# A two-layer transformer kernel in fp32 on one core: block 1 of the feed-forward part joins the seven-product scheme, with its weight sums made early and the later high parts cast by ScalarE

## The chip, the cores and the metric

One core of one Trainium2 chip runs the whole program. The metric is device time in microseconds, the median of several executions.

## The reference

Input `x` is 2 x 1024 x 512, fp32. Four stages follow one another: attention a, feed-forward, attention b, feed-forward. Each adds to its own input what it computes from the layer-normed input:

```python
x = x + attn_a(layernorm(x), W_qkv, b_qkv, W_out, b_out)   # 16 heads, causal
x = x + ffn(layernorm(x), w_gate, w_up, w_down)
x = x + attn_b(layernorm(x), w_qkv, b_qkv, w_proj, b_proj)
x = x + ffn(layernorm(x), w_gate, w_up, w_down)            # the same ffn weights

def ffn(x, w_gate, w_up, w_down):       # 512 -> 2048 -> 512
    return (silu(x @ w_gate.T) * (x @ w_up.T)) @ w_down.T
```

## The kernel before

The kernel makes four passes (two batch entries of 1024 tokens, two layers each). A pass is one attention and one feed-forward part. Every product is made to nearly fp32 precision from rounded numbers: an operand is split into a high part (rounded to fp32r) and a low part (what is left), and the function `three` issues three matmuls, high by high, high by low, low by high (L1166 to L1168).

**Feed-forward in blocks.** The 2048 hidden units are 8 blocks of 256. A block comes as three weight slots of 128 x 1024 numbers: gate, up and down. The 1024 tokens are two chunks of 512. A step `s` is a block and a chunk (`s = 2 * block + chunk`); 16 steps. In a plain block, `gate_up(s, t)` computes 128 hidden units for 512 tokens, gate and up, and `down_row(s, t)` adds the block's share of 128 tokens of output to one PSUM bank. Gate and up of a plain block are 96 matmuls of 512 columns, down is 48.

**Seven products.** For blocks `QUAD_FIRST` to `QUAD_LAST`, 2 to 6 in the kernel before, gate and up are made in a scheme with seven block products instead of eight (Strassen's, in Winograd's form): the weights are cut in 2 x 2 (two halves of the 512 inputs, two of the 256 hidden units), and so are the layer-normed tokens (inputs, chunk). Four sums of weight parts and four sums of token parts (`diff`, once per pass) replace some of the operands. The products are called `m1` to `m7` and come in the order m1, m7, m6, m5, m3, m4, m2; each is made twice, for gate (w = 0) and for up (w = 1), 6 matmuls each time, so 84 for a block. Outputs are named (t, c): half of the hidden units, chunk. PSUM has few banks, so m1, m6 and m5 are copied out by ScalarE (`keep`) and added back by VectorE (`quad_add`). Rows of the down projection of the step before are put behind m7, m6 and m5 (`ROWS_BEHIND`).

**Who does what around it.** There is no planner; each engine has its list written out by hand, and semaphores with counts order them.
- SyncE loads the weight slots into `w_stage` (two places). Slot i is loaded once slot i - 2 is split (`w_split`).
- GpSimd (POOL) takes the slots in order. For a gate or up slot of a seven-product block it first makes the four sums (`quad_sums`, L547 to L552) and splits them (`s_split`: a cast at L558 makes the high part, a subtraction at L561 the low part); then it splits the slot (`split_weights`: cast L528, subtraction L530). Before the down slot of block 1 it makes the six token sums (`diff_sum`, L578). It waits for a place of the `area` to come free from `last_product`.
- ScalarE (ACT) applies silu, makes the high part of each hidden tile (`hidden_hi` L765, `quad_hi` L773), keeps products (L746), and casts the four token sums (`diff_to_hi`, L738), one behind each hidden tile of steps 1 and 2.
- VectorE (DVE) multiplies, makes low parts (`hidden_parts` L1029 and L1035, `quad_lo` L1000), adds rows to `x` (L967), and makes the low parts of the token sums (`diff_to_lo`, L974) behind the hidden tiles of steps 2 and 3. Around the last output projection it normalises the last attention unit (L935) and splits it (L942, L944), which TensorE needs for its last four products.
- TensorE (PE) waits for `w_split` before a block's products, for `h_ready` before m2 (the low part of output (1, 1)), for `product_kept` before m6, m5 and m3, and for `diff_ready` in the first block of the scheme.

In ScalarE's list of a seven-product block the six `keep` come first, and then, for each output in the order (1, 1), (0, 1), (1, 0), (0, 0), `quad_silu` and `quad_hi`.

The sums of weights lie in memory lent by the attention part. `s_parts` and `s_sums` give the place number n of a slot, (2 * (b - QUAD_FIRST) + w) % 4: parts 1, 2, 3 of `area` (key buffers of the attention), and a fourth place in `kq_parts` and `xt_late`. `quad_sums` of the first block of the scheme waits until the attention's last score tile is read (`s2_full`).

Of the kernel before, what the change touches and what calls it, by code (L numbers as in the profile page):

```python
# [27 lines left out]
ALU = mybir.AluOpType  # L28
ACT = mybir.ActivationFunctionType

P = 128
# [16 lines left out]
STEPS = BLOCKS * CHUNKS  # L48


QUAD_FIRST, QUAD_LAST = 2, BLOCKS - 2
QUADS = QUAD_LAST - QUAD_FIRST + 1
QUAD_STEPS = range(2 * QUAD_FIRST, 2 * QUAD_LAST + 2)

# [8 lines left out]
ROW_STEPS = (*range(2 * QUAD_FIRST), *(2 * b + 1 - c for b in range(QUAD_FIRST, QUAD_LAST) for c in range(2)),  # L63
             *range(2 * QUAD_LAST, STEPS))

SLOT = 1024
V_SLOTS, QK_SLOT0, WO_SLOT0, FFN_SLOT0 = (0, 1), 2, 2 + GROUPS, 4 + GROUPS
SLOTS = FFN_SLOT0 + 3 * BLOCKS
# [9 lines left out]
ATTN_PLACES = (2, 4, 3, 3, 2, 4, 3, 2)  # L78
FFN_PLACES = (4, 1, 0, 3, 2)
AHEAD = QK_SLOT0 + 1  # L80
DIFF_STEPS = (2, 3)
DIFFS_AT = FFN_SLOT0 + 5


# [97 lines left out]
def block_kernel(nc, x_in, attn_w, ffn_w, qk_bias, row_bias, out):  # L182
    with ExitStack() as ctx:
# [146 lines left out]
        def s_parts(b, w):  # L330

            n = (2 * (b - QUAD_FIRST) + w) % 4
            if n == 3:
                return kq_parts[:, :, :].rearrange("p (r h) (i n) -> p r (h i) n", r=2, n=2 * P)
            return area[:, 1 + n, :].rearrange("p (r i n) -> p r i n", r=2, n=2 * P)

        def s_sums(b, w):

            n = (2 * (b - QUAD_FIRST) + w) % 4
            lo = xt_late[:, 2:4, :].rearrange("p h n -> p (h n)") if n == 3 else area_f32[:, 1 + n, SLOT:2 * SLOT]  # L340
            return lo.rearrange("p (i n) -> p i n", n=2 * P)

        def rows_taken(it, row):
# [47 lines left out]
        def wait_alone(eng, semaphore, value):  # L391


            if not isinstance(value, int):
                value = eng.snap(eng.to_reg(value))
            eng.wait_ge(const_ready, CONSTS)
            eng.wait_ge(semaphore, value)
# [100 lines left out]
        def _(pool):  # L498
            def split_weights(it, i):

                j = i % SLOTS
                n = it * SLOTS + i
                wait_alone(pool, w_loaded[j % 2], (it * (SLOTS // 2) + i // 2 + 1) * 16)

                b, part = divmod(j - FFN_SLOT0, 3)
                if part < 2 and QUAD_FIRST <= b <= QUAD_LAST:
                    quad_sums(it, b, part, w_stage[:, j % 2, :])
                    s_split(it, b, part)

                before = slot_before(j)  # L510
                if i >= SLOTS:
                    before = max(q for q in range(SLOTS) if place(q) == place(j))
                if before is not None:
                    after = last_product(before)
                    if after[0] == "product":
                        wait_alone(pool, product_full, products(it, *after[1:]))
                    elif after[0] == "rows":
                        wait_alone(pool, rows_full, it * ROWS + after[1] + 1)
                    elif after in SIDE:
                        wait_alone(pool, side_full, side_done(it, after))  # L520
                    else:
                        wait_alone(pool, ring_full, full(it, after))
                elif place(j) in LENT_PLACES:

                    lent_steps = KEY_STEPS if place(j) == 0 else J_BASE[6]
                    wait_alone(pool, s2_full, it * S2_STEPS + GH * lent_steps)
                hi, lo, src = *w_part(j, slice(0, SLOT)), w_stage[:, j % 2, :]
                pool.tensor_scalar(hi, src, 1.0, 0.0, ALU.mult, ALU.add).then_inc(w_hi_done, 1)  # L528
                pool.wait_ge(w_hi_done, n + 1)
                pool.tensor_tensor(lo, src, hi.bitcast(F32), ALU.subtract).then_inc(w_split, 1)  # L530
# [5 lines left out]
            def quad_sums(it, b, w, src):  # L536

                a = src.rearrange("p (k f) -> p k f", f=BLOCK)
                a11, a12, a21, a22 = (a[:, k:k + 2, f:f + P] for f in (0, P) for k in (0, 2))
                if b >= QUAD_FIRST + 2:  # L540
                    wait_alone(pool, product_full, products(it, b - 2, "m3", w))
                elif b == QUAD_FIRST + 1 and w == 1:
                    wait_alone(pool, diff_step, it * 6 + 4)
                elif b == QUAD_FIRST:
                    wait_alone(pool, s2_full, it * S2_STEPS + GH * KEY_STEPS)
                s1, s2, s3, s4 = (s_sums(b, w)[:, i, :].rearrange("p (k f) -> p k f", f=P) for i in range(4))
                pool.tensor_tensor(s1, a21, a22, ALU.add).then_inc(s_step, 1)  # L547
                pool.tensor_tensor(s3, a11, a21, ALU.subtract).then_inc(s_step, 1)
                wait_alone(pool, s_step, s_steps(it, b, w, 0))
                pool.tensor_tensor(s2, s1, a11, ALU.subtract).then_inc(s_step, 1)  # L550
                wait_alone(pool, s_step, s_steps(it, b, w, 2))
                pool.tensor_tensor(s4, a12, s2, ALU.subtract).then_inc(s_step, 1)  # L552

            def s_split(it, b, w):

                both, sums = s_parts(b, w), s_sums(b, w)
                wait_alone(pool, s_step, s_steps(it, b, w, 3))
                pool.tensor_scalar(both[:, 0, :, :], sums, 1.0, 0.0, ALU.mult, ALU.add  # L558
                                   ).then_inc(s_step, 1)
                wait_alone(pool, s_step, s_steps(it, b, w, 4))  # L560
                pool.tensor_tensor(both[:, 1, :, :], sums, both[:, 0, :, :].bitcast(F32),  # L561
                                   ALU.subtract)
# [70 lines left out]
            with pool.Fori(0, BATCH * LAYERS) as it:  # L633
# [12 lines left out]
                for u in range(UNITS):  # L646
# [8 lines left out]
                    for d in range(CT):  # L655
                        mask_probs(it, u, d)
                        if u == UNITS - 1 and d == 0:
                            inverse_deviation(it, 1, 0)
                split_weights(it, FFN_SLOT0 + 2)
                inverse_deviation(it, 1, 1)  # L660

                wait_alone(pool, xn_ready, it * 2 * TT + 2 * TT)
                for i in range(FFN_SLOT0 + 3, SLOTS + 2):
# [15 lines left out]
        def _(act):  # L679
# [11 lines left out]
            def iteration(it):  # L691
# [43 lines left out]
                def diff_to_hi(i):  # L735

                    act.wait_ge(diff_step, it * 6 + (1, 3, 4, 6)[i])
                    act.activation(diff_hi[:, i, :, :], diff_f32[:, i, :, :], ACT.Copy  # L738
                                   ).then_inc(diff_hi_done, 1)

                def keep(b, m, w):

                    if b > QUAD_FIRST:
                        act.wait_ge(h_ready, low_count(it, b - 1, ADDED[("m5", "m6", "m1").index(m)]))
                    act.wait_ge(product_full, products(it, b, m, w))
                    act.activation(kept[m][:, w, :], quad_bank("x", w), ACT.Copy).then_inc(product_kept, 1)  # L746
# [56 lines left out]
                    hidden_hi(0, t)  # L803
                xt_to_hi(it, ("ln2", 2))
                xt_to_hi(it, ("ln2", 3))
                for s in range(1, QUAD_STEPS[0]):
                    for t in range(BT):
                        silus(s, t)
                        hidden_hi(s, t)
                        if s in (1, 2):  # L810
                            diff_to_hi((s - 1) * BT + t)
                for b in range(QUAD_FIRST, QUAD_LAST + 1):
                    for m in KEPT:
                        for w in range(2):
                            keep(b, m, w)
                    for which in OUTPUTS:
                        quad_silu(b, which)
                        quad_hi(b, which)
                for s in range(QUAD_STEPS[-1] + 1, STEPS):
                    for t in range(BT):  # L820
# [20 lines left out]
        def _(dve):  # L841
# [41 lines left out]
            def iteration(it, b, layer):  # L883
# [118 lines left out]

                def quad_block(b):
                    add_rows(2 * b - 1)
                    if b > QUAD_FIRST:
                        add_rows(2 * b - 2, range(2))
                    quad_add(b, (1, 1), 0)
                    quad_add(b, (1, 1), 1)
                    quad_multiply(b, (1, 1))
                    if b > QUAD_FIRST:  # L1010
                        add_rows(2 * b - 2, range(2, CT))
                    quad_lo(b, (1, 1))
                    quad_multiply(b, (0, 1))
                    quad_lo(b, (0, 1))
                    for which in ((1, 0), (0, 0)):
                        quad_add(b, which, 0)
                        quad_add(b, which, 1)
                        quad_multiply(b, which)
                        quad_lo(b, which)
# [84 lines left out]
                xt_to_lo(it, 1, 2)  # L1104
                xt_to_lo(it, 1, 3)
                add_rows(0)
                for s in range(1, QUAD_STEPS[0]):
                    for t in range(BT):
                        hidden_parts(s, t)
                        if s in DIFF_STEPS:  # L1110
                            diff_to_lo(BT * DIFF_STEPS.index(s) + t)
                    for d in downs_after(s):
                        add_rows(d)
                for block_at in range(QUAD_FIRST, QUAD_LAST + 1):
# [450 lines left out]
```

## Time and profile before

| | |
|---|---|
| median of 3 executions | 2128.01 us (2127.96 to 2130.42) |
| profiled execution, its own time | 2130.63 us |
| its span, first to last instruction | 2128.9 us |
| mean granted TensorE clock | 0.995 |
| busy share PE, VectorE, ScalarE, GpSimd | 97%, 57%, 33%, 47% |
| instructions of TensorE | 10816 matmuls |

Times in rows are microseconds from the span's start. An engine's busy time is the sum over its instructions; matmuls overlap one another in it, so PE's pace is read from start to start. The span has four passes that are nearly alike, and the feed-forward part of the first one lies between about 291 and 530 us.

### The profile page before, as it was taken

What the parts mean: (1) busy time and instruction counts of PE and PEld (TensorE: products, weight loads), DVE (VectorE), ACT (ScalarE), POOL (GpSimd) and SP (SyncE); (2) the same over time, 40 slices, a digit from 0 to 9 for tenths busy, and PEclk for the clock granted to TensorE, in tenths of its full rate; (3) what the DMA queues carried; (4) which work ended last, traced back from release to release, by engine and by line L of the source; (5) the groups of instructions that cost most, each with busy time, mean ns of one, the idle gap of its engine ahead of it and who ended that gap; (6) DMA issues with size and microseconds to landing.
All of it is one profiled execution on the core that took longest, in us unless ns stands there. A gap on an engine that the chain in (4) does not pass through costs nothing.

```text
span 2128.9 us, 35275 instructions
## 1 busy us (share of the span) xinstructions
PE 2062.0 (97%) x10816; PEld 1443.1 (68%) x10816; DVE 1210.9 (57%) x2452; ACT 698.6 (33%) x1348; POOL 999.1 (47%) x776
## 2 busy tenths in 40 slices
PE   6999999999999999999999999999999999999997
PEld 5555478888755547888875554888877554588886
DVE  6766554454676645544557664555456666454554
ACT  1344432231144443222214444222221444422321
POOL 3323249863312425975331242697533223379752
PEclk9999999999999999999999999999999999999999
DMA  4433101111323210211242321111113232111112
GB/s 129 101 78 83 32 30 50 60 60 40 81 71 81 71 31 30 64 51 55 70 131 71 81 71 31 40 60 50 50 41 85 66 81 71 41 39 62 50 57 92
DMA packets 59756, 135.18 MB, mean 63 GB/s; under 512 B 10784, under 2 KB 11808, under 8 KB 59552
## 3 DMA queue, kind: packets, MB, share of 16 engines
q1 hardware_dynamic: 59552, 132.71, 22.1%
q8 instruction: 98, 1.61, 0.3%
q14 instruction: 106, 0.87, 0.1%
HBM read 77.62 MB, written 4.19 MB: 38 GB/s over the span
## 4 chain that ended last, share of the span: by engine, by line
PE 86%; issue 4%; DVE 3%; POOL 3%; ACT 2%; DMA 1%; SPq 0%; DVEq 0%; POOLq 0%; ACTq 0%
PE bank L1279 13%; PE bank L1166 10%; PE bank L1168 10%; PE bank L1167 10%; PE ring L1166 9%; PE ring L1167 9%; PE ring L1168 9%; PE ring L1233 8%; PE bank L1257 7%; PE ring L1157 1%; POOL area L671 1%; ACT prob L713 1%; DMA area<-nm_lo 1%; POOL area L530 1%; DVE xn L908 1%
## 5 line engine op out<-in xcount | busy, mean ns | idle before, releaser
L713 ACT ACTIVATE prob<-bank 128x512 f32<-128x512 f32 (+3 forms) x768 | 335.0, 489 | 343.6 <-PE bank L1257 342.8
L908 DVE CUSTOM_DVE_ANT_0 xn<-ring,mask_row 128x128 bf16<-128x128 f32 (+7 forms) x512 | 374.8, 749 | 106.4 <-PE ring L1233 99.5
L605 POOL TENSOR_SCALAR_AFFINE_SELECT prob<-prob 128x512 f32<-128x512 f32 x128 | 84.1, 657 | 568.7 <-ACT prob L713 568.7
L528 POOL TENSOR_SCALAR area<-w_stage 128x1024 fp32r<-128x1024 f32 x131 | 149.9, 1144 | 369.3 <-PE bank L1168 194.7
L530 POOL TENSOR_TENSOR area<-w_stage,area 128x1024 fp32r<-128x1024 f32 x131 | 313.9, 2396 | 10.9
L967 DVE TENSOR_TENSOR x<-x,bank 128x512 f32<-128x512 f32 x256 | 170.8, 684 | 233.1 <-PE bank L1168 233.1
L1166 PE MATMUL ring<-xt_hi,area 128*128 128x512 f32 x688 | 273.7, 398 | 4.3 <-DVE xt_lo L880 2.8
L1167 PE MATMUL ring<-xt_lo,area 128*128 128x512 f32 x688 | 269.3, 391 | 0.0
L1168 PE MATMUL ring<-xt_hi,area 128*128 128x512 f32 x688 | 268.9, 391 | 0.0
L1233 PE MATMUL ring<-area 96*128 96x512 f32 (+3 forms) x768 | 239.1, 372 | 9.4 <-DVE row_max L908 8.4
L1233 PEld LDWEIGHTS ring<-area 96*128 96x128 f32 x768 | 131.1, 188 | 151.1 <-DVE row_max L908 94.5
L1257 PE MATMUL bank<-area 98*128 98x512 f32 (+3 forms) x768 | 225.5, 372 | 7.9 <-DMA area<-nm_lo 4.0
L1257 PEld LDWEIGHTS bank<-area 98*128 98x128 f32 x768 | 125.5, 189 | 123.4 <-ACT prob L713 94.5
L1166 PE MATMUL bank<-area 128*128 128x512 f32 x512 | 200.5, 392 | 0.3 <-DVE area L1035 0.2
L1168 PE MATMUL bank<-area 128*128 128x512 f32 x512 | 199.3, 389 | 0.0
L1167 PE MATMUL bank<-area 128*128 128x512 f32 x512 | 199.3, 389 | 0.0
L1279 PE MATMUL bank<-prob,v 128*32 128x512 f32 (+3 forms) x1536 | 165.3, 502 | 9.1 <-POOL prob L605 7.3
L1279 PE MATMUL bank<-prob,ones 128*32 128x512 f32 (+3 forms) x1536 | 163.1, 496 | 0.0
L1166 PEld LDWEIGHTS ring<-xt_hi,area 128*128 128x128 f32 x688 | 129.6, 188 | 43.8 <-issue 9.8
L1168 PEld LDWEIGHTS ring<-xt_hi,area 128*128 128x128 f32 x688 | 129.6, 188 | 27.9
L1167 PEld LDWEIGHTS ring<-xt_lo,area 128*128 128x128 f32 x688 | 129.9, 189 | 25.4
L929 DVE RECIPROCAL recip<-recip 128x64 f32<-128x64 f32 x256 | 123.8, 522 | 15.0 <-ACT attn L723 15.0
(144 smaller groups left out, 3233.6 us busy)
## 6 DMA issues: line engine op xcount, KB each, us to landing
w_stage<-ffn_w SPq DMA_DIRECT2D x96, 512.0 KB, 3.3
area<-kq_parts SPq DMA_DIRECT2D x336, 128.0 KB, 2.4
w_stage<-attn_w SPq DMA_DIRECT2D x35, 512.0 KB, 3.2
x<-x_in SPq DMA_DIRECT2D x24, 256.0 KB, 3.9
area<-attn SPq DMA_DIRECT2D x48, 128.0 KB, 2.3
out<-x SPq DMA_DIRECT2D x16, 256.0 KB, 2.1
bias_rows<-row_bias SPq DMA_DIRECT2D x10, 256.0 KB, 4.2
area<-nm_hi SPq DMA_DIRECT2D x32, 8.0 KB, 1.8
```

What stands on the lines that cost most here:

```text
L528: pool.tensor_scalar(hi, src, 1.0, 0.0, ALU.mult, ALU.add).then_inc(w_hi_done, 1)
L530: pool.tensor_tensor(lo, src, hi.bitcast(F32), ALU.subtract).then_inc(w_split, 1)
L713: act.activation(prob[:, step % 2, h, off:], bank[n % 2][:, off:], ACT.Exp, scale=SCALE).then_inc(prob_ready, 1)
L908: dve.tensor_tensor_reduce(out=sum_out[:, RING[name] % 2, 0:keys], in0=src[:, 0:keys], in1=mask_row[:, TOKENS - keys:], scale=1.0, scalar= ...
L929: dve.reciprocal(recip[:, cols], recip[:, cols]).then_inc(recip_done, 1)
L967: dve.tensor_tensor(x[:, t, :], x[:, t, :], row_bank(s, n)[:, :], ALU.add).then_inc(rows_drained, 1)
L1166: pe.matmul(dst, ah, bh, start=first and k == 0, stop=False, skip_group_check=more)
L1167: pe.matmul(dst, ah, bl, start=False, stop=False, skip_group_check=more)
L1168: ins = pe.matmul(dst, al, bh, start=False, stop=last and k == n - 1, skip_group_check=more)
L1233: ins = pe.matmul(buffer_of(("s1", u, s))[:, kc, 0:n], q, k_stack[0:3 * HEAD, keys_of(u, kc), h, 0:n], start=True, stop=True)
L1257: pe.matmul(bank[n % 2][:, off:], k_stack[rows, keys_of(u, j // CT), h, j % CT * P:(j % CT + 1) * P], q_stack[rows, q_buffer(u), h, off:], ...
L1279: ins = pe.matmul(dst[rows, off:], a, prob[:, step % 2, h, off:], start=j == 0, stop=j == key_tiles(u) - 1, tile_position=(0, h * HEAD))
```

## The change

Three things. First, `QUAD_FIRST` goes from 2 to 1, so that six blocks, 1 to 6, use seven products. Second, the order of the token sums and the weight sums of block 1 moves: the gate sums of block 1 are made and split by GpSimd directly behind the split of the down slot of block 0, ahead of the second chunk's inverse deviation; the token sums' high and low parts are made behind the second transposed half, behind the two tiles of step 1, and inside block 1. The lent places are used in another order (`S_AREAS`), so that the first two only need an earlier attention unit to be done. Third, from the second seven-product block on, ScalarE and not GpSimd casts the high part of the weight sums: for gate behind keeping m6 of the block before, for up between the silu and the high part of its output (1, 1).

```diff
-QUAD_FIRST, QUAD_LAST = 2, BLOCKS - 2
+QUAD_FIRST, QUAD_LAST = 1, BLOCKS - 2
+SUMS_BEHIND = ("m6", (1, 1))
-DIFF_STEPS = (2, 3)
+S_AREAS = (2, 3, 1)
+EARLY_SUMS = True
...
         def s_parts(b, w):
-            return area[:, 1 + n, :].rearrange("p (r i n) -> p r i n", r=2, n=2 * P)
+            return area[:, S_AREAS[n], :].rearrange("p (r i n) -> p r i n", r=2, n=2 * P)
         def s_sums(b, w):
-            lo = xt_late[:, 2:4, :].rearrange("p h n -> p (h n)") if n == 3 else area_f32[:, 1 + n, SLOT:2 * SLOT]
+            lo = xt_late[:, 2:4, :].rearrange("p h n -> p (h n)") if n == 3 else area_f32[:, S_AREAS[n], SLOT:2 * SLOT]
...
 GpSimd, split_weights
-                if part < 2 and QUAD_FIRST <= b <= QUAD_LAST:
+                if part < 2 and QUAD_FIRST <= b <= QUAD_LAST and j != FFN_SLOT0 + 3:
                     quad_sums(it, b, part, w_stage[:, j % 2, :])
                     s_split(it, b, part)
 GpSimd, quad_sums
-                elif b == QUAD_FIRST:
+                elif b == QUAD_FIRST + 1:
                     wait_alone(pool, s2_full, it * S2_STEPS + GH * KEY_STEPS)
+                else:
+                    wait_alone(pool, s2_full, it * S2_STEPS + GH * J_BASE[6])
 GpSimd, s_split
-                pool.tensor_scalar(both[:, 0, :, :], sums, 1.0, 0.0, ALU.mult, ALU.add
-                                   ).then_inc(s_step, 1)
+                if b == QUAD_FIRST:
+                    pool.tensor_scalar(both[:, 0, :, :], sums, 1.0, 0.0, ALU.mult, ALU.add
+                                       ).then_inc(s_step, 1)
 GpSimd, the pass
                 split_weights(it, FFN_SLOT0 + 2)
+                wait_alone(pool, w_loaded[1], (it * (SLOTS // 2) + (FFN_SLOT0 + 3) // 2 + 1) * 16)
+                if EARLY_SUMS:
+                    quad_sums(it, 1, 0, w_stage[:, 1, :])
+                    s_split(it, 1, 0)
                 inverse_deviation(it, 1, 1)
+                if not EARLY_SUMS:
+                    wait_alone(pool, xn_ready, it * 2 * TT + 2 * TT)
+                    quad_sums(it, 1, 0, w_stage[:, 1, :])
+                    s_split(it, 1, 0)
 ScalarE
+                def sums_to_hi(b, w):
+                    if b > QUAD_LAST:
+                        return
+                    act.wait_ge(s_step, ((it * QUADS + b - QUAD_FIRST) * 2 + w) * 5 + 4)
+                    act.activation(s_parts(b, w)[:, 0, :, :], s_sums(b, w), ACT.Copy).then_inc(s_step, 1)
...
                 xt_to_hi(it, ("ln2", 3))
+                diff_to_hi(0)
                 for s in range(1, QUAD_STEPS[0]):
                     for t in range(BT):
                         silus(s, t)
                         hidden_hi(s, t)
-                        if s in (1, 2):
-                            diff_to_hi((s - 1) * BT + t)
+                        diff_to_hi(1 + t)
                 for b in range(QUAD_FIRST, QUAD_LAST + 1):
                     for m in KEPT:
                         for w in range(2):
                             keep(b, m, w)
+                        if m == SUMS_BEHIND[0]:
+                            sums_to_hi(b + 1, 0)
+                        if b == QUAD_FIRST and m == KEPT[0]:
+                            diff_to_hi(3)
                     for which in OUTPUTS:
                         quad_silu(b, which)
+                        if which == SUMS_BEHIND[1]:
+                            sums_to_hi(b + 1, 1)
                         quad_hi(b, which)
 VectorE
                 def quad_block(b):
                     add_rows(2 * b - 1)
+                    if b == QUAD_FIRST:
+                        diff_to_lo(3)
...
                 add_rows(0)
+                diff_to_lo(0)
                 for s in range(1, QUAD_STEPS[0]):
                     for t in range(BT):
                         hidden_parts(s, t)
-                        if s in DIFF_STEPS:
-                            diff_to_lo(BT * DIFF_STEPS.index(s) + t)
+                        diff_to_lo(1 + t)
```

## Rows read from the trace of the kernel before

**Rows 1.** The page's engine shares: busy us, share of the span, instructions.
```profile
PE 2062.0 (97%) x10816; PEld 1443.1 (68%) x10816; DVE 1210.9 (57%) x2452; ACT 698.6 (33%) x1348; POOL 999.1 (47%) x776
```

**Rows 2.** Busy time by engine from step 1 to block 2, first pass.
```profile
core 0: us, PE busy (x) PEld busy (x) DVE busy (x) ACT busy (x) POOL busy (x), PEclk, DMA share, GB/s
309.70:353.10 43.40, 43.33 (x191) 35.90 (x192) 22.10 (x25) 10.98 (x16) 41.59 (x25) 1.00 0.10 28
```

**Rows 3.** Timeline of PE: start, length, instruction; step 1, down rows, block 2.
```profile
279.78 0.50 PE L1166 MATMUL bank<-area,xt_hi 128*128 128x512 f32 x1
...
309.77 0.49 PE L1166 MATMUL ring<-xt_hi,area 128*128 128x512 f32 x1 [0.70 <-DVE xt_lo L880]
...
347.98 0.39 PE L1166 MATMUL bank<-area 128*128 128x512 f32 x1
...
353.42 0.42 PE L1166 MATMUL bank<-xt_hi,area 128*128 128x512 f32 x1
```

**Rows 4.** Timeline of POOL, from the last split before the FFN to block 2.
```profile
280.26 2.41 POOL L530 TENSOR_TENSOR area<-w_stage,area 128x1024 fp32r<-128x1024 f32 x1
295.09 1.01 POOL L598 TENSOR_TENSOR rstd<-var_eps,minus_half 128x4 f32<-128x4 f32 x1 [12.43 <-DVE var_eps L857]
298.53 1.05 POOL L528 TENSOR_SCALAR area<-w_stage 128x1024 fp32r<-128x1024 f32 x1 [2.42 <-DVE attn L871]
...
302.02 1.05 POOL L528 TENSOR_SCALAR area<-w_stage 128x1024 fp32r<-128x1024 f32 x1
...
309.79 2.41 POOL L578 TENSOR_TENSOR attn<-xt_late 128x1024 f32<-128x1024 f32 x1 [4.22 <-DVE xt_lo L880]
...
324.65 1.06 POOL L528 TENSOR_SCALAR area<-w_stage 128x1024 fp32r<-128x1024 f32 x1
...
329.55 1.72 POOL L550 TENSOR_TENSOR area_f<-area_f,w_stage 128x256 f32<-128x256 f32 x1
...
340.37 0.74 POOL L547 TENSOR_TENSOR area_f<-w_stage 128x256 f32<-128x256 f32 x1
...
343.54 1.05 POOL L558 TENSOR_SCALAR area<-area_f 128x1024 fp32r<-128x1024 f32 x1 [0.16 <-POOL area_f L552]
...
347.10 2.04 POOL L528 TENSOR_SCALAR area<-w_stage 128x1024 fp32r<-128x1024 f32 x1
349.21 2.40 POOL L530 TENSOR_TENSOR area<-w_stage,area 128x1024 fp32r<-128x1024 f32 x1
```

**Rows 5.** Timelines of POOL and DVE: where they meet; split of the last attention unit.
```profile
140.23 2.38 POOL L530 TENSOR_TENSOR area<-w_stage,area 128x1024 fp32r<-128x1024 f32 x1
...
141.91 1.25 DVE L935 TENSOR_TENSOR attn<-attn,recip 128x512 f32<-128x512 f32 x1
...
284.58 0.69 DVE L935 TENSOR_TENSOR attn<-attn,recip 128x512 f32<-128x512 f32 x1
...
285.77 0.69 DVE L944 TENSOR_TENSOR xt_lo<-attn,xt_hi 128x512 fp32r<-128x512 f32 x1
...
329.02 1.66 DVE L974 TENSOR_TENSOR diff_lo<-attn,diff_hi 128x1024 fp32r<-128x1024 f32 x1
...
345.35 2.87 DVE L974 TENSOR_TENSOR diff_lo<-attn,diff_hi 128x1024 fp32r<-128x1024 f32 x1
```

**Rows 6.** Timelines of ACT and DVE: a cast of 1024, high and low part of an output.
```profile
333.72 1.05 ACT L738 ACTIVATE diff_hi<-attn 128x1024 fp32r<-128x1024 f32 x1
...
372.76 0.60 ACT L773 ACTIVATE area<-ring 128x512 fp32r<-128x512 f32 x1 [0.79 <-DVE ring L995]
373.39 0.69 DVE L1000 TENSOR_TENSOR area<-ring,area 128x512 fp32r<-128x512 f32 x1 [0.67 <-ACT area L773]
```

**Rows 7.** PE and its granted clock around the end of the second pass.
```profile
1084.12 1.97 PE L1157 MATMUL ring<-ident,xn 128*128 128x128 f32 x8 [2.53 <-DVE xn L871]
...
1088.58 0.63 PE L1168 MATMUL ring<-xt_hi,area 128*128 128x512 f32 x1
...
1084.00:1090.80 6.80, 6.48 (x19) 5.12 (x20) 4.12 (x8) 1.02 (x1) 0.00 (x0) 0.50 0.02 4
```

## The prediction

> **What bounds the kernel now.** I read the page's engine shares first [rows 1]: PE is busy in 2062.0 of 2128.9 us, so whatever is taken from PE's list of work and not replaced by a wait comes off the time. Then the stretch from the second transposed half of the second layer norm to the first seven-product block, by engine [rows 2]: PE 43.33 of 43.40 us at full clock, and POOL 41.59 of 43.40. Both are full. VectorE (22.10) and ScalarE (10.98) are not. That is the one stretch that the change rebuilds, so the question is which of the two full engines ends last after it. All four layer passes have the same FFN; I work with the first one and multiply by 4.
>
> PE's pitch comes from the 24 matmuls of one step of the down projection, 347.98 to 353.42: 0.2267 us each [rows 3]. From 309.77 (gate and up of step 1, which waits for the last `xt_lo`) to 353.42 there are 192 matmuls, 43.5 us, plus 0.1 for the restart: no other hole. POOL's own list is in [rows 4]. One weight slot split (cast 1.05, subtract 2.4) takes 3.5 us (298.53 to 302.02). Sums and their split, measured where nothing disturbs them (340.37 to 347.10), take 6.73, of which the four sums are 3.0 (343.54 less the 0.16 gap). The six differences take 14.86 (309.79 to 324.65). POOL stands idle for 4.2 us ahead of 309.79. After that it has no hole, and the up slot of block 2 is ready at 351.6 (349.21 and 2.40), for a product that starts at 354.8 (6 matmuls behind 353.42): 3.2 us of slack.
>
> **The change, part by part.**
>
> *Block 1 goes to seven products.* Gate and up of a block are 96 matmuls in the plain form and 84 in the seven-product form: 12 x 0.2267 = 2.72 us less, 10.9 us in four passes. The down projection has as many matmuls as before. This is all the gain there is.
>
> *What else moves on PE.* Between 309.87 and the second product m1 of block 2 (up weights) there stood 198 matmuls: steps 1, 2, 3, the down rows of 1 and 2, and one m1. Now there are 48 (step 1), 84 (block 1), 24 (rows of step 1) and 6: 162. Rows of steps 2 and 3 move behind. So PE arrives there at 309.87 + 162 x 0.2267 = 346.6, 8.2 us earlier than before. It arrives at m2 of block 1 after 144 matmuls, at 342.5.
>
> *Sums of block 1, gate part, made early.* They come behind the split that ends at 282.67 [rows 4] and take 6.73, to 289.4; the next thing POOL does is the variance at 295.09. On POOL they cost nothing. But they now lie beside three VectorE operations with two SBUF inputs or a doubled rate, L935, L942 and L944, at 284.58 to 286.46 [rows 5], ahead of the last output projection. In this place POOL is idle today. The nearest row of such a meeting is L935 at 141.91: 1.25 us, against 0.69, beside a POOL subtraction that ends at 142.61 [rows 5]. It waited until then. Step by step with 0.74 us sums: L935 waits for the sum that ends at 284.75 and ends at 285.45, one sum comes between, the cast ends at 286.5, POOL's own cast comes between, L944 ends at 288.1. PE has 36 matmuls from 279.78, so it needs this at 287.95: 0.2 of wait, with the restart 0.3. Bounds: 0 if the operations miss each other, 2.4 if the last one meets a whole subtraction.
>
> *Sums of block 1, up part.* 6.73 us on POOL behind the split of the gate slot. They fill the hole of 4.2, the rest (2.5) pushes the differences and everything behind.
>
> *Differences to high and low parts.* Four ScalarE casts (1.05) and four VectorE subtractions L974, moved into step 1 and between. In the trace L974 lasts 1.66 to 2.87 and each one holds one POOL operation up: L550 1.72 against 0.74, L528 2.04 against 1.05, so 1.0 each [rows 4, 5]. Three of these fall before 351.6 today; four fall before the same point in the new order. VectorE's order now has the first L974 ahead of the hidden product of step 1, and it waits for the third difference step (about 319.6): hidden parts of step 1 are done at 322.8 and 326.3, the third difference at 327.9. PE wants them at 323.5, 326.2 and 327.6. These are waits of some tenths, and they vanish in the larger one below.
>
> The Trainium skill, page "SBUF — State Buffer", section "SBUF: two separate sides", says that GpSimd and a VectorE operation with two SBUF inputs or in a two-port mode take a shared port pair as a lock for a whole instruction, the other one waiting. The rows above agree. By that rule all four L974 cost POOL their 1.0; without it the list below would end 4 us earlier in each pass, and the time would be that of the second rival.
>
> *ScalarE casts the high parts of block 2 and on.* This takes 1.05 off POOL and gives it a wait for an equal cast on ScalarE (L738 is 1.05 [rows 6]); POOL gains nothing, as its subtraction needs the result. What is new is a wait in ScalarE's queue. The gate cast stands ahead of keeping m5, and PE's m3 waits for that. The up cast stands between the silu of output (1, 1) and its high part, and PE's m2 waits for that.
>
> *POOL's new list from 298.53.* Split 3.5, sums and split 6.73, split 3.5: 312.25, later than the transposed half is ready, so no idle. Differences 14.86: 327.1. Split 3.5, gate sums and split of block 2 6.73, split 3.5: 340.85. Up sums 3.0: 343.85. Four hold-ups of 1.0: 347.85.
>
> *What PE then waits for.* ScalarE's up cast runs 347.9 to 348.95, the high part 0.60 to 349.5, the low part 0.69 (the pair L773, L1000 [rows 6]) to 350.2. PE wanted m2 at 342.5. It has waited some 2 us at m3 and m4 by then (the gate sums end at 336.7, the cast at 337.8, m5 kept at 338.35 against 337.5; the last difference low part waits for POOL's subtraction until 340.3, so m4 starts at 342.1 against 341.2), and these are part of the 7.7, not beside it. Last, the up slot of block 2: 347.85 + 1.15 (cast) + 2.45 + 3.5 = 355.0, against 346.6. PE is 8.4 us late there. With three hold-ups it is 7.4, with none 4.4.
>
> *Does it come back?* No. PE's list is fixed and nothing later was waiting. From block 3 on there is no new loss: one block is 132 matmuls, 29.9 us, of PE, and POOL needs 3 x 3.5 + 2 x 6.73 = 24.0 and a wait at the gate cast. The up slot of block 3 is then ready near 382.5 for a product at 385.1.
>
> *The clock.* Ahead of 1084.12 PE is idle for 2.5 us, and the granted clock is 0.50 for the 6.8 us that follow, 1.2 GHz and not 2.4; a matmul of 512 columns lasts 0.63 there instead of 0.39 [rows 7]. The new wait at m2 is one hole of about 5 us. If the clock falls, m2 and m1 lose up to 1.7 of the first 3.4 us, of which 0.6 lies under the wait for the up slot. I take 0.7 per pass (bounds 0 and 3). The Trainium skill, "TensorE: Matmul & The Clock Gate", section "HAM oscillation — how this bites in real kernels", names waits for an input as what sends the clock down again; with no fall at all the forecast would be 3 us lower.
>
> **Sum per pass:** -2.72 + 8.4 + 0.3 + 0.7 = +6.7 us; four passes +26.7. The profiled execution took 2130.6 (span 2128.9), 2.6 above the median shown of 2128.0. 2130.6 + 26.7 = 2157.3 by the profile, 2154.7 by the median; I forecast 2155.
>
> **Rivals.**
>
> *Worse than that.* L944 meets the whole subtraction of POOL (2.4 instead of 0.3) and the clock stays low for 6.8 us (2 instead of 0.7): +3.4 per pass on top, 2168; one of the two gives 2160 to 2163. For: the lengths of the queue in [rows 4] make the order of L944 and POOL's next operation a matter of 0.1 us. Against: by my times it meets the cast.
>
> *POOL is less held up.* The L974 fall into POOL's own gaps or into its waits for ScalarE, at most none counts: +4.4 instead of 8.4, no long hole, clock stays: -2.72 + 4.4 + 0.1 = +1.8, 2135. For: the fourth may well fall into the wait for the gate cast. Against: today all four are paid.
>
> *Faster.* POOL keeps up, the seven-product form is paid in full: 2128.0 - 10.9 = 2117. The mechanism would be POOL's up slot of block 2 ready ahead of PE. It decides at 346.6 for the full gain and at 349.3 for any; by the list even with no hold-up it is 351.0. It needs something in the list to be 2 us shorter than its rows, against 45 us of measured rows. For: the early sums really are free, and POOL is at 47% over the whole span [rows 1].
>
> *No change* would need a displacement of just 2.7, between the last two.
>
> **How the numbers follow.** Forecast 0.60, worse 0.15, less held up 0.12, faster 0.10, no change 0.03. A measurement of this kernel tells about 0.2%, 4 us. So faster 0.10, same 0.03, slower 0.87. The range leaves out the faster cases and the far ends of the others: 2133 to 2164. The likeliest case's own range is 2148 to 2160.
>
> **What would show it.** PE: some 12 x 4 matmuls fewer, and a hole of about 5 us ahead of m2 of block 1, released by a VectorE low part, with ScalarE's sum cast and POOL's four sums just ahead of it. POOL: no idle of over 1 us from 298.5 until the up slot of block 2 is split at about 355. VectorE: L944 ends at about 288. A clock of 0.50 behind the hole. It would be wrong if the up slot of block 2 were split before 349, if the hole stood at m1 of block 2 alone, or if later blocks had holes as well.

## The result, and the profile after

The changed kernel takes 2158.69 us, the median of 4 executions (2157.39 to 2159.43), against 2127.99 (2127.96 to 2130.42): a ratio of 1.0134, 95% interval 1.0122 to 1.0147. It is slower by 30.7 us; forecast were 2155 and a range of 2133 to 2164. Its profiled execution took 2158.3 (span 2156.6), 27.7 more than that of before.

The stretch from step 1 to the second last step of the FFN is cut out of each pass by two marks that both kernels have: the restart behind the last `xt_lo` and the restart ahead of step 14. The view by windows gives length, busy time of PE, its weight loads, DVE, ACT and POOL, then the granted clock. Before, then after; four passes each.

```profile
309.77:498.15 188.38, 188.04 (x829) 155.29 (x829) 92.20 (x131) 51.17 (x84) 144.40 (x104) 1.00 0.16 51
832.27:1020.63 188.36, 188.03 (x829) 155.28 (x829) 92.23 (x131) 51.17 (x84) 144.39 (x104) 1.00 0.15 51
...
1882.82:2071.23 188.41, 188.08 (x829) 155.29 (x829) 92.38 (x131) 51.16 (x84) 144.41 (x104) 1.00 0.15 51
```

```profile
310.48:505.38 194.90, 188.44 (x817) 154.04 (x817) 94.53 (x137) 63.55 (x100) 136.12 (x96) 0.98 0.15 52
839.43:1034.44 195.01, 188.53 (x817) 154.07 (x817) 94.51 (x137) 63.55 (x100) 136.16 (x96) 0.98 0.16 52
1375.59:1570.31 194.72, 188.22 (x817) 153.88 (x817) 94.53 (x137) 63.55 (x100) 136.14 (x96) 0.99 0.16 52
1904.59:2099.32 194.73, 188.23 (x816) 153.89 (x816) 94.52 (x137) 63.56 (x100) 136.12 (x96) 0.99 0.16 52
```

Twelve matmuls are gone from each pass (the profile has one record fewer in the last), and the stretch is 6.3 to 6.7 us longer, 25.8 in all. The remaining 1.9 of the 27.7 lies between the stretches of the second and the third pass (341.15 us against 339.25, clock 0.98 against 0.99). Some 1.6 of it stands in the attention there, code that the change doesn't touch: TensorE runs at the lower clock for 3.4 us from about 1313.7, and was never idle for over 0.45 us just ahead of it:

```profile
1313.60:1317.00 3.40, 3.40 (x18) 0.70 (x10) 0.00 (x0) 1.41 (x3) 3.23 (x4) 0.51 0.00 0
```

POOL's list in the first pass, the changed kernel (L530 and L532 split a slot, L551 to L556 make the four sums, L563 and L566 split them, L583 makes the token differences). It answers to [rows 4]:

```profile
280.93 2.41 POOL L532 TENSOR_TENSOR area<-w_stage,area 128x1024 fp32r<-128x1024 f32 x1
283.29 0.73 POOL L551 TENSOR_TENSOR area_f<-w_stage 128x256 f32<-128x256 f32 x1
...
287.93 2.64 POOL L566 TENSOR_TENSOR area<-area_f,area 128x1024 fp32r<-128x1024 f32 x1
295.79 1.02 POOL L603 TENSOR_TENSOR rstd<-var_eps,minus_half 128x4 f32<-128x4 f32 x1 [5.22 <-DVE var_eps L883]
299.24 1.06 POOL L530 TENSOR_SCALAR area<-w_stage 128x1024 fp32r<-128x1024 f32 x1 [2.42 <-DVE attn L897]
...
302.73 0.73 POOL L551 TENSOR_TENSOR area_f<-w_stage 128x256 f32<-128x256 f32 x1
...
317.84 2.39 POOL L583 TENSOR_TENSOR attn<-attn,xt_lo 128x1024 f32<-128x1024 f32 x1
320.38 3.38 POOL L583 TENSOR_TENSOR attn<-xt_late,attn 128x1024 f32<-128x1024 f32 x1
...
345.32 0.73 POOL L551 TENSOR_TENSOR xt_late<-w_stage 128x256 f32<-128x256 f32 x1
...
347.55 0.72 POOL L556 TENSOR_TENSOR xt_late<-w_stage,xt_late 128x256 f32<-128x256 f32 x1
349.51 2.37 POOL L566 TENSOR_TENSOR kq_parts<-xt_late,kq_parts 128x1024 fp32r<-128x1024 f32 x1 [1.23 <-ACT kq_parts L759]
...
352.97 2.39 POOL L532 TENSOR_TENSOR area<-w_stage,area 128x1024 fp32r<-128x1024 f32 x1
```

The last line is the up slot of block 2, split at 355.36. The pass starts 0.7 later in this execution, so that is 354.7 on the clock of before; the sum said 355.0. No idle time of over 1.3 us lies between 299.24 and it; the two longest, 1.24 and 1.23, are the waits for ScalarE's casts. The chain to TensorE, ScalarE's list (L759 casts sums, L793 makes the high part of an output):

```profile
342.61 0.63 ACT L778 ACTIVATE xn<-xn 128x512 f32<-128x512 f32 x1 [3.27 <-DVE xn L1011]
348.31 1.06 ACT L759 ACTIVATE kq_parts<-xt_late 128x1024 fp32r<-128x1024 f32 x1 [5.07 <-POOL xt_late L556]
349.27 0.58 ACT L793 ACTIVATE area<-ring 128x512 fp32r<-128x512 f32 x1
```

VectorE's (L961, L968 and L970 are the three of [rows 5] beside the early sums; L1000 is a token low part, L1026 an output's):

```profile
285.25 0.71 DVE L961 TENSOR_TENSOR attn<-attn,recip 128x512 f32<-128x512 f32 x1
286.00 0.84 DVE L968 CAST xt_hi<-attn 128x512 fp32r<-128x512 f32 x1
286.88 1.44 DVE L970 TENSOR_TENSOR xt_lo<-attn,xt_hi 128x512 fp32r<-128x512 f32 x1
...
320.27 1.23 DVE L1000 TENSOR_TENSOR diff_lo<-attn,diff_hi 128x1024 fp32r<-128x1024 f32 x1 [7.53 <-POOL attn L583]
...
339.17 2.81 DVE L1000 TENSOR_TENSOR diff_lo<-attn,diff_hi 128x1024 fp32r<-128x1024 f32 x1
...
349.88 0.69 DVE L1026 TENSOR_TENSOR area<-ring,area 128x512 fp32r<-128x512 f32 x1 [5.88 <-ACT area L793]
```

And TensorE's: m4 of block 1, the hole, m2, then m1 of block 2:

```profile
342.72 0.47 PE L1194 MATMUL ring<-diff_hi,area 128*128 128x512 f32 x1 [0.81 <-DVE xn L1011]
...
345.32 0.39 PE L1196 MATMUL ring<-diff_hi,area 128*128 128x512 f32 x1
350.63 0.80 PE L1194 MATMUL ring<-xt_hi,area 128*128 128x512 f32 x1 [4.92 <-DVE area L1026]
...
353.78 0.63 PE L1195 MATMUL ring<-xt_lo,area 128*128 128x512 f32 x1
...
355.28 0.39 PE L1194 MATMUL bank<-xt_hi,area 128*128 128x512 f32 x1
```

```profile
350.60:354.50 3.90, 3.87 (x9) 3.11 (x10) 3.11 (x5) 1.23 (x2) 3.82 (x3) 0.50 0.00 0
```

Behind the hole nine of the twelve matmuls of m2 run at the lower clock, 1.2 GHz. TensorE then reaches the up m1 of block 2 at 356.6, later than its slot (355.4), so the slot makes no second hole.

### The profile page after: what moved, and what is told of

Its sections match the earlier page's. It is cut to its first block, busy times and chain, and to the rows that moved or that the text cites. A ratio compares the mean times of both kernels' runs of the same rounds, so it can differ in the third digit from the quotient of the medians.

```text
span 2156.6 us, 35523 instructions
## 1 busy us (share of the span) xinstructions
PE 2064.6 (96%) x10768; PEld 1437.8 (67%) x10768; DVE 1224.9 (57%) x2476; ACT 748.3 (35%) x1412; POOL 1008.0 (47%) x784
## 4 chain that ended last, share of the span: by engine, by line
PE 74%; POOL 9%; issue 9%; DVE 4%; ACT 2%; DMA 1%; POOLq 1%; SPq 0%; DVEq 0%; ACTq 0%
PE bank L1307 13%; PE bank L1196 9%; PE bank L1194 9%; PE bank L1195 9%; PE ring L1261 8%; PE bank L1285 7%; PE ring L1194 7%; PE ring L1195 6%; PE ring L1196 6%; POOL attn L583 3%; POOL area L530 1%; POOL area L684 1%; PE ring L1185 1%; POOL area L532 1%; ACT prob L726 1%
## 5 line engine op out<-in xcount | busy, mean ns | idle before, releaser
L532 POOL TENSOR_TENSOR area<-w_stage,area 128x1024 fp32r<-128x1024 f32 x131 | 314.0, 2397 | 10.9
L530 POOL TENSOR_SCALAR area<-w_stage 128x1024 fp32r<-128x1024 f32 x131 | 141.6, 1081 | 299.7 <-PE bank L1196 154.6
L1194 PE MATMUL ring<-xt_hi,area 128*128 128x512 f32 x576 | 233.3, 405 | 24.8 <-DVE area L1026 21.0
L1195 PE MATMUL ring<-xt_lo,area 128*128 128x512 f32 x576 | 228.8, 397 | 0.0
L1196 PE MATMUL ring<-xt_hi,area 128*128 128x512 f32 x576 | 228.2, 396 | 0.0
L1194 PEld LDWEIGHTS ring<-xt_hi,area 128*128 128x128 f32 x576 | 110.5, 192 | 62.0 <-DVE area L1026 24.4
L566 POOL TENSOR_TENSOR area<-area_f,area 128x1024 fp32r<-128x1024 f32 x36 | 87.4, 2427 | 122.2 <-ACT area L759 121.0
L1196 PEld LDWEIGHTS ring<-xt_hi,area 128*128 128x128 f32 x576 | 110.4, 192 | 24.1
```

The costliest lines, as they stand in the source:

```text
L1194: pe.matmul(dst, ah, bh, start=first and k == 0, stop=False, skip_group_check=more)
L1195: pe.matmul(dst, ah, bl, start=False, stop=False, skip_group_check=more)
L1196: ins = pe.matmul(dst, al, bh, start=False, stop=last and k == n - 1, skip_group_check=more)
```

## The experiments

Each ratio is to the kernel before as it was executed beside the experiment: 2128.2 us for experiments 1 to 4, 2130.3 for 5 to 7, 2130.6 for 8 and 9.

**1. The casts back on GpSimd.**

```diff
 GpSimd, s_split
-                if b == QUAD_FIRST:
-                    pool.tensor_scalar(both[:, 0, :, :], sums, ...)
+                pool.tensor_scalar(both[:, 0, :, :], sums, ...)
 ScalarE: both calls of sums_to_hi left out
```

> The changed kernel, but GpSimd itself casts the high parts of all weight sums, as in the kernel before; ScalarE casts none. Theory A (GpSimd's list ahead of the up slot of block 2 is what TensorE waits for): the list keeps its length, since a cast of 1.05 us replaces a wait for a cast of 1.05 us. The hole ahead of m2 of block 1 goes, and an equal one stands at the second m1 of block 2, where TensorE waits for the up slot until about 355.3 in the first pass: 2155 to 2161 us, no difference to 2158.7 that counts. Rival B (the place of the up cast in ScalarE's queue makes the hole): 5.1 us of hole less in each pass and nothing in its place, about 2138 us.

2159.59 us (2159.26 to 2161.35), ratio 1.0148 (1.0131 to 1.0165). The time is in the range of theory A, 21 us above that of rival B. The hole left m2 and stood at the second m1 of block 2, ahead of which GpSimd's list ended:

```profile
342.22 0.47 PE L1189 MATMUL ring<-diff_hi,area 128*128 128x512 f32 x1 [1.59 <-DVE xn L1006]
...
355.03 0.79 PE L1189 MATMUL bank<-xt_hi,area 128*128 128x512 f32 x1 [5.70 <-POOL area L532]
```

**2. ScalarE's up cast one place later.**

```diff
-                        if which == SUMS_BEHIND[1]:
-                            sums_to_hi(b + 1, 1)
                         quad_hi(b, which)
+                        if which == SUMS_BEHIND[1]:
+                            sums_to_hi(b + 1, 1)
```

> The changed kernel with ScalarE's up cast one place later: behind the high part of output (1, 1), so that m2 no longer depends on it. Theory A: m2 of block 1 starts without the 5 us hole, and TensorE waits the same time in front of m1 of block 2: 2156 to 2161 us. Rival B: the order on ScalarE is the cause, 2138 us.

2156.25 us (2152.78 to 2158.24), ratio 1.0127 (1.0110 to 1.0144): the interval contains the changed kernel's 1.0134. The hole moved to m1 of block 2:

```profile
352.73 0.80 PE L1194 MATMUL bank<-xt_hi,area 128*128 128x512 f32 x1 [3.58 <-DVE area L1026]
```

Here TensorE still waits through ScalarE's queue, since the other outputs stand behind the cast; in experiment 1 ScalarE has no cast at all. Rival B, which said 2138 for both, falls: who is named as TensorE's releaser changes with the order on ScalarE (a VectorE low part, or POOL), the time hardly does.

**3. The gate sums of block 1 late.**

```diff
-EARLY_SUMS = True
+EARLY_SUMS = False
```

> The changed kernel with the gate sums of block 1 made behind the inverse deviation, where the rest of GpSimd's list begins (the early place switched off). Theory A: GpSimd's list from 299.2 to the up slot of block 2 is longer by the 6.73 us of four sums and their split, and TensorE is later by the same: 4 x 6.7 = 27 us more, about 2185 us. Rival C (GpSimd's list has room, the holes come from hand-offs between engines): within 5 us of 2158.7.

2184.76 us (2183.14 to 2185.64), 26.1 more than the changed kernel, with 26.9 said. POOL's list is longer by the sums' own 6.73. Its up slot of block 2 is split at 360.4 in a pass that starts at 308.99, so 6.5 us later in the pass than in the changed kernel, and TensorE is 6.5 a pass later:

```profile
357.99 2.41 POOL L532 TENSOR_TENSOR area<-w_stage,area 128x1024 fp32r<-128x1024 f32 x1
```

The rival of a list with room (C) falls, and the early sums are shown to be worth what they take. There is a second hole now, at m7 of block 1, where TensorE waits for step 1's hidden tile behind the late differences:

```profile
328.52 0.80 PE L1194 MATMUL ring<-diff_hi,area 128*128 128x512 f32 x1 [5.63 <-DVE area L1063]
```

**4. The kernel before with ScalarE's casts alone.**

```diff
 to the kernel before
 GpSimd, s_split:  + if b == QUAD_FIRST:   (the cast)
 ScalarE:          + sums_to_hi(b + 1, 0) behind keeping m6
                   + sums_to_hi(b + 1, 1) between quad_silu and quad_hi of (1, 1)
```

> The kernel before with one part of the change alone: ScalarE casts the high parts of the summed weights from the second seven-product block on (blocks 3 to 6), gate behind keeping m6, up between the silu and the high part of output (1, 1). Theory A: GpSimd has room in these blocks (24 us of work in 29.9), so the casts' place costs nothing: 2126 to 2130 us. Rival B: each hand-off holds an output's high part up, 1 us in each of 4 blocks and 4 passes, about 2144 us.

2135.01 us (2132.39 to 2136.90), ratio 1.0032 (1.0021 to 1.0044): 6.8 us slower, so the first expectation failed, and the rival's 2144 too. The loss is in one place of each pass, block 2, the first of the scheme there:

```profile
359.26 0.74 POOL L552 TENSOR_TENSOR area_f<-w_stage,area_f 128x256 f32<-128x256 f32 x1
365.81 2.40 POOL L562 TENSOR_TENSOR area<-area_f,area 128x1024 fp32r<-128x1024 f32 x1 [5.81 <-ACT area L747]
```

```profile
377.04 0.50 PE L1178 MATMUL ring<-xt_hi,area 128*128 128x512 f32 x1 [0.72 <-DVE area L1012]
...
381.86 0.50 PE L1178 MATMUL bank<-xt_hi,area 128*128 128x512 f32 x1 [0.40 <-POOL area L530]
```

POOL's gate sums of block 3 are done at 360.0, but ScalarE's cast stands behind keeping m6 of block 2 and ends at 365.7. POOL is 5.8 us idle and is then late for the up slot. The gaps of 1.1 and 0.8 us between matmul starts are 1.4 us over the pitch, and the stretch of a pass is 190.1 to 190.2 us against 188.4, so 7.0 in four passes.

The expectation set POOL's 24 us against 29.9 us of block. But the first block of the scheme has only the 24 down rows' matmuls of one step beside its 84, 108 and not 132. In the kernel before, block 2 starts at 353.42 [rows 3], blocks 3 and 4 like this:

```profile
377.97 0.39 PE L1166 MATMUL bank<-xt_hi,area 128*128 128x512 f32 x1
...
407.89 0.39 PE L1166 MATMUL bank<-xt_hi,area 128*128 128x512 f32 x1
```

Block 2 lasts 24.6 us, block 3 29.9. Without its two casts POOL's work in a block is 24.0 less 2.1, so 21.9 us; with the waits of 5.8 and 1.2 for ScalarE it needs some 28.9 (an estimate from these rows). That fits into 29.9 and not into 24.6, and the slack of 3.2 us at block 2 doesn't cover it.

**5 to 7. The token differences on VectorE.** VectorE was busy for half of the stretch [rows 2], and does one in 1.2 to 1.8 us (experiment 6, first pass) where POOL takes 2.39.

```diff
 GpSimd
-                        for n in range(6):
-                            diff_sum(it, n)
 VectorE, behind add_rows(0)
+                dve.wait_ge(ring_drained, drained(it, ("ln2", 3)))
+                for n in range(5):
+                    diff_sum(dve, it, n)
                 diff_to_lo(0)
 VectorE, behind the two tiles of step 1
+                    diff_sum(dve, it, 5)
```

The first has just this, the second also the casts back on GpSimd as in experiment 1, the third those casts and only the first four differences on VectorE.

> The changed kernel, but VectorE makes all six token differences (5 behind the rows of step 0, the last behind the hidden tiles of step 1), and GpSimd none. ScalarE's casts stay. Theory A: GpSimd's list ahead of the up slot of block 2 is shorter by 14.9 us less the new idle time until gate and up of step 1 have left their weights (321.6), so its slot comes at 348 to 350 instead of 355.4, for a product that can start at 347.3. A rest of 1 to 2 us per pass stays through the hand-off of the casts, as in the kernel before with casts on ScalarE (1.8): 2122 to 2128 us. Rival D (the 5 us hole comes from the new place of the token parts on VectorE and ScalarE, not from GpSimd): VectorE gets 7 us more to do there, 2165 us or more.

> As the one before, and GpSimd casts the weight sums itself, so that no output's high part stands behind them. Theory A: GpSimd from 321.6: slot 3.5, gate sums and split 6.7, slot 3.5, up sums and split 6.7, slot 3.5: 345.5, and up to four hold-ups of 1 us by VectorE; TensorE wants it at 347.3. So 0 to 2.3 us of hole per pass and nearly the whole gain of 2.7: 2117 to 2127 us, likely 2121, faster than both kernels. Rival D: 2165 us.

> As the one before, but only the first four differences on VectorE, the last two on GpSimd. Theory A: they lie partly in GpSimd's new idle time ahead of 321.6 and put its list back by 2 to 3 us: TensorE waits 2 to 4 us per pass, 2125 to 2133 us. Rival E (VectorE is the bound once it makes the differences): this one is faster than the one with all six on VectorE.

2130.83 us (ratio 1.0004, 0.9995 to 1.0014), 2132.99 (1.0016, 1.0007 to 1.0025) and 2136.73 (1.0029, 1.0019 to 1.0038). Some 22 to 28 us of the loss are gone with 15 us less on POOL's list (10 in the third), and rivals D and E fall: none is near 2165, and the third is slower than the second. The up slot comes only 5.3 us earlier in the pass, since POOL now stands idle for 8.8 us until TensorE has left the place of the next weights (experiment 6).

But none beats the kernel before, and all three missed their ranges from above: 2130.8 for 2122 to 2128, 2133.0 for 2117 to 2127, 2136.7 for 2125 to 2133. In the first, the clock does not fall in the stretch, which takes 188.3 us in each pass, as long as before; the kernel before itself stood 2.1 us higher in these executions (2130.3) than in those of experiments 1 to 4, which is most of the miss of 2.8. In the other two TensorE waits 2.3 us at the second m1 of block 2, the edge of what was said for the second, and then comes what was left out of these expectations, the clock. One pass of the second did not have the fall:

```profile
348.91 0.71 PE L1189 MATMUL bank<-xt_hi,area 128*128 128x512 f32 x1 [2.32 <-POOL area L548]
349.41 0.63 PE L1190 MATMUL bank<-xt_lo,area 128*128 128x512 f32 x1
```

```profile
309.36:499.37 190.01, 187.36 (x817) 154.00 (x817) 100.88 (x143) 54.49 (x90) 132.39 (x100) 0.99 0.16 53
833.57:1021.94 188.37, 185.72 (x817) 152.82 (x817) 100.87 (x143) 54.37 (x90) 132.34 (x100) 1.00 0.16 54
```

190.0 with 3.4 us at the lower clock behind the hole, 188.4 without: one fall costs 1.6 us. The hole stands in both. In the third kernel the clock fell in all four passes of its profiled execution, 190.9 us each.

**8 and 9. GpSimd's order within a slot.** The slot itself is split before its sums are, since m1 needs only the slot; the sums' parts are first used by m7.

```diff
 GpSimd, split_weights
                 quad_sums(it, b, part, w_stage[:, j % 2, :])
-                s_split(it, b, part)
                 ...                                  (the slot's own cast and subtraction)
+                s_split(it, b, part)                 (its subtraction now counts up s_ready)
 TensorE, product
                 elif m == "m7":
+                    pe.wait_ge(s_ready, (it * QUADS + b - QUAD_FIRST) * 2 + w + 1)
```

The first is made from the second kernel of the last group, the other from experiment 1 (all on GpSimd).

> As the one with all differences on VectorE and all casts on GpSimd, and GpSimd's order within a slot changed: four sums, then the split of the slot itself, then the split of the sums; TensorE waits for the split of the sums at m7, by a semaphore of its own, not at m1. Theory A: the up slot of block 2 comes 3.7 us earlier (the split of the sums follows it), 345.3 instead of 348.9, for a product at 346.2; the sums' low part is ready at about 349, for the up product m7 at 350.3. No hole, no fall of the clock: four times the 2.7 us of the twelve matmuls, 2116 to 2121 us. Rival F (the mere length of GpSimd's list counts, the order within it does not): the hole of 2.5 us stays in front of m7, 2131 to 2134 us.

> The changed kernel with all casts and all differences on GpSimd, and the same new order: sums, slot, split of the sums, with TensorE's wait at m7. Theory A: the wait at the up m1 of block 2 shrinks by 3.7 us, and at the up m7, four us of TensorE work later, the sums' low part is as late as the up slot was: the displacement goes from some 8 us per pass to some 5, 2143 to 2150 us. Rival F: no difference to 2159.6.

The first takes 2115.98 us (2115.12 to 2116.35), ratio 0.9936 (0.9922 to 0.9950): faster than both kernels, and at the lower edge of what was said. The second takes 2138.40 (2138.32 to 2142.45), 21 us less than with the old order (experiment 1), more than said (9 to 16), so it missed its range (2143 to 2150). Its waits are shorter than experiment 1's by 3.6 us at the up m1, and its clock does not fall in the FFN, which it did in each pass there (196.4 us for the stretch against 190.9). With POOL's list as long as before, the rival of mere length (F) falls. In the first POOL has the up slot of block 2 split at 345.5, and TensorE starts on it at 347.5 without a wait:

```profile
343.13 2.40 POOL L549 TENSOR_TENSOR area<-w_stage,area 128x1024 fp32r<-128x1024 f32 x1
```

The stretch of the first, and its profile's shares:

```profile
310.32:496.24 185.92, 185.57 (x816) 152.98 (x816) 101.02 (x143) 54.39 (x90) 131.80 (x99) 1.00 0.17 54
```

```profile
PE 2047.7 (97%) x10768; PEld 1431.5 (68%) x10768; DVE 1250.5 (59%) x2500; ACT 711.5 (34%) x1372; POOL 991.0 (47%) x800
```

185.9 is 2.5 less than the 188.4 of before: the 2.7 us of the twelve matmuls, less one restart.

## Why the prediction was right, by its steps

- **The gain.** Right: 829 matmuls are 817, and where nothing waits that is 2.5 us a pass.
- **POOL's list.** Right as a sum: 355.0 said, 354.7 measured. The four hold-ups of 1.0 came as told: three differences L583 last 3.38 against 2.39, and one L530 lasts 2.02 against 1.05. The Trainium skill, "SBUF — State Buffer", section "SBUF: two separate sides", has a GpSimd operation and a VectorE operation with two SBUF inputs, as L1000 is, lock each other out for a whole instruction; these rows agree.
- **The hole at m2.** Right in place and size: 4.92 us, with 0.8 at m4 ahead of it. m2 starts at 350.63, 349.9 on the clock of before, against the 350.2 said. Experiments 1 and 2 show that ScalarE's queue only decides which instruction shows POOL's lateness; experiments 3, 6 and 9 show the lateness itself.
- **The early sums.** They were to cost 0.3 at the last output projection. L970 ended at 288.3 (287.6 on the clock of before, needed at 287.95) and nothing waited: 0. L968 and L970 did wait for POOL, 0.4 and 0.75 us.
- **The clock.** It fell in all four passes, for 6.8 us in the first two, of which half lies in the hole, and for 3.4 in the others. Per pass 0.7 was taken. Since nine matmuls of m2 run slow, TensorE comes 1.3 us behind the slot instead of 0.6 ahead of it. A fall costs 1.6 by experiment 6, and more of it lies open than was taken: this makes up for the 0.3 that wasn't there. That the two errors cancel is luck.
- **The sum.** 6.7 a pass said, 6.3 to 6.7 measured.
- **Later blocks.** Right for the changed kernel: no hole behind block 2. The reason given (24 us of work in 29.9) holds from block 2 of the changed kernel on. It does not hold for the first block of the scheme, which lasts 24.6 us, as experiment 4 shows.
- **The 4 us between 2155 and 2158.7.** The subtraction of 2.6 for the profiled execution was not borne out: the profiled execution of the changed kernel lies 0.4 under its median, not 2.6 over it. That is 3.0; another 1.0 is the 27.7 measured against 26.7.

The rival of less holding up (2135) failed since all four hold-ups were paid. The faster one needed the slot at 346.6. Experiment 8 gets it there by other means.

## What to carry to other kernels

Taking work off a full engine makes it ask for its inputs earlier: add up the supplier's whole list to the moved deadline, not its busy share. A hole shows up at whatever stands next in the consumer's queue, so test the name in the trace by moving it. And before moving work to another engine, look at what the first consumer needs and put that first in the supplier's list.

## What the runs showed of the hardware

Holes of one size were followed by a fall of TensorE's clock or not. The hole of 2.3 us in experiment 6 was followed by 3.4 us at the lower clock in three of four passes and not in the second; that of 2.3 us in experiment 7 in all four; that of 2.1 us in experiment 9 in none. In experiment 2 the clock fell in three passes, and stayed at full speed in the third (1.00 over the stretch) behind a hole of 3.6 us:

```profile
1415.31 0.50 PE L1194 MATMUL bank<-xt_hi,area 128*128 128x512 f32 x1 [3.61 <-DVE area L1026]
```

It also fell with hardly any hole ahead of it, in the attention of both kernels: at 1313.7 in the changed kernel, as shown above, and at about 770 in the kernel before (idle 0.45 and 0.21 us just ahead). What decides is open. The kernel before, which has no long wait in its feed-forward blocks, took from 2125.6 to 2133.5 us in the 27 executions beside experiments 5 to 7, with a mean granted clock from 0.997 down to 0.993.
